# A transformer block on one core: the last MLP bias by an accumulating DMA, and one head moved from GpSimd to VectorE

## The reference

```python
x = x + attn_block(layernorm(x))
x = x + ffn(layernorm(x))

def attn_block(q_x):                      # q_x: normalized tokens
    xn = ln(q_x) * ln1_w + ln1_b
    q, k, v = xn @ wq + bq, xn @ wk + bk, xn @ wv + bv        # 16 heads of 16
    fq, fk = elu(q) + 1, elu(k) + 1
    # per token, over its heads h and the 16 x 16 features:
    kv    = einsum('bhnd,bhne->bnde', fk, v)
    attn  = einsum('bhnd,bnde->bhne', fq, kv) / (einsum('bhnd,bnd->bhn', fq, fk.sum(heads)) + 1e-6)
    x = q_x + attn @ wo + bo
    h = gelu((ln(x) * ln2_w + ln2_b) @ fc_w + fc_b)            # MLP 256 -> 1024
    return x + (h @ proj_w + proj_b)                           # MLP 1024 -> 256, the bias of this change

def ffn(x):                               # 8 experts, best two per token, and a shared MLP
    return silu(x @ sg_gate.T) * (x @ sg_up.T) @ sg_down.T + sum over two experts of weight * expert(x)
```

## Time and profile before

| what | value |
|---|---|
| median of three runs | 1758.97 us (1758.11 to 1759.81) |
| the profiled execution | 1756.6 us, of it 1754.7 us span |
| TensorE (PE) busy | 1682.2 us, 96% |
| VectorE (DVE) busy | 1176.5 us, 67% (nine tenths and more in the block loop) |
| GpSimd (POOL) busy | 1166.0 us, 66% |
| ScalarE (ACT) busy | 903.8 us, 52% |
| chain that ended last | PE 87%, ACT 5%, DVE 4%, issue 2% |
| DMA engines | mean 90 GB/s, one tenth busy in the block loop |

### The profile page before, as it was taken

The page is one execution under the profiler, slowest core; times in us unless marked ns, Lnnn a source line. Parts: engine busy times, 40 slices in busy tenths (PEclk is TensorE's granted clock), DMA queues, the critical chain, the costliest instruction groups (busy, mean ns, idle before and its releaser), DMA issues.

```text
span 1754.7 us, 25629 instructions
## 1 busy us (share of the span) xinstructions
PE 1682.2 (96%) x7243; PEld 1230.4 (70%) x7289; DVE 1176.5 (67%) x1967; ACT 903.8 (52%) x2240; POOL 1166.0 (66%) x624
## 2 busy tenths in 40 slices
PE   5888999999999999999999997989999999999997
PEld 3655665665665665665665664668888888888886
DVE  7999999999999999999999992222222222222221
ACT  4266667667667667667667636522232232232232
POOL 4779889889899899899889891314333333333333
PEclk9998999999999999999999998999999999999999
DMA  4211111111111111111111111166776766767774
GB/s 150 75 51 63 49 51 47 50 57 40 48 53 43 48 47 49 48 50 47 48 42 55 37 48 37 55 199 154 160 167 153 161 165 153 162 164 154 165 161 78
DMA packets 89455, 157.20 MB, mean 90 GB/s; under 512 B 8896, under 2 KB 72128, under 8 KB 89024
## 3 DMA queue, kind: packets, MB, share of 16 engines
q1 hardware_dynamic: 60512, 112.58, 20.6%
q0 software_dynamic: 28896, 44.06, 14.7%
HBM read 101.79 MB, written 48.56 MB: 86 GB/s over the span
## 4 chain that ended last, share of the span: by engine, by line
PE 87%; ACT 5%; DVE 4%; issue 2%; DMA 1%; SPq 1%; POOL 0%; POOLq 0%; ACTq 0%; DVEq 0%
PE p_b L1484 18%; PE p_b L1538 13%; PE p_b L1688 10%; PE p_b L1699 10%; PE p_b L1631 9%; PE p_q L1688 7%; PE p_q L1456 6%; PE p_v L1688 4%; PE p_v L1456 3%; PE p_b L1470 2%; PE p_xT L1675 2%; ACT rows L706 1%; ACT xmid L706 1%; PE p_xT L1616 1%; DVE prod L1014 1%
## 5 line engine op out<-in xcount | busy, mean ns | idle before, releaser
L654 POOL DMA_INDIRECT out_rows<-prod_pool,prod x142 | 221.2, 1558 | 385.8 <-ACT prod_pool L937 355.4
L523 POOL TENSOR_TENSOR prod_pool<-prod_pool 128x2048 f32<-128x2048 f32 (+1 forms) x180 | 347.6, 1931 | 15.1 <-DVE attn L1064 1.1
L1538 PE MATMUL p_b<-bT,fc_sb 128*128 128x512 f32 x512 | 231.1, 605 | 1.3 <-ACT bT L858 1.3
L1484 PE MATMUL p_b<-proj_sb,hid 128*128 128x256 f32 x1024 | 230.5, 379 | 0.0
L1484 PEld LDWEIGHTS p_b<-proj_sb,hid 128*128 128x128 f32 x1024 | 189.7, 190 | 29.4 <-issue 0.5
L1688 PE MATMUL p_b<-prod,exp_up 128*128 128x256 f32 x840 | 187.1, 379 | 0.0
L1014 DVE TENSOR_TENSOR prod<-p_q,eqk 128x4096 f32<-128x4096 f32 (+1 forms) x47 | 184.0, 3914 | 4.6
L1051 DVE TENSOR_REDUCE qkv<-prod 128x256 f32<-128x4096 f32 (+1 forms) x47 | 183.7, 3910 | 1.6
L1038 DVE TENSOR_TENSOR prod<-p_q,v_dve 128x2048 f32<-128x2048 f32 (+2 forms) x60 | 177.4, 2956 | 1.6
L1023 DVE TENSOR_REDUCE p_q<-prod 128x128 f32<-128x2048 f32 (+2 forms) x60 | 177.4, 2957 | 1.1
L574 POOL DMA_INDIRECT rows_sorted<-rows,slot x128 | 125.3, 979 | 79.0 <-issue 34.5
(11 more groups left out here) (207 smaller groups left out, 3005.3 us busy)
## 6 DMA issues: line engine op xcount, KB each, us to landing
exp_up<-in_experts SPq DMA_DIRECT2D x71, 768.0 KB, 4.6
prod<-rows_sorted SPq DMA_DIRECT2D x71, 260.0 KB, 2.8
xin<-in_x SPq DMA_DIRECT2D x16, 512.0 KB, 3.4
xres<-in_x SPq DMA_DIRECT2D x16, 512.0 KB, 3.8
xres<-xmid POOLq DMA_DIRECT2D x16, 512.0 KB, 4.6
out_rows<-x SPq DMA_DIRECT2D x16, 512.0 KB, 2.9
exp_dn<-in_experts SPq DMA_DIRECT2D x8, 384.0 KB, 5.5
out_rows<-prod_pool,prod POOLq DMA_INDIRECT x142, 3.8
```

The costliest lines, as they stand in the source:

```text
L523: done(g.tensor_tensor(prod_pool[:, at:at + n * w], prod_pool[:, at:at + n * w], prod_pool[:, at + n * w:at + 2 * n * w], ALU.add))
L654: pool.indirect_dma_start(out=out[:, :], out_offset=bass.IndirectOffsetOnAxis(ap=tok_i[j][:, a:a + 1], axis=0), in_=yg[j][:, a * D:(a + 1) ...
L1484: ins = t_.matmul(o, src[:, k, t * P:(t + 1) * P], w[:, k, :], start=k == 0, stop=bias_at is None and k == chunks - 1)
L1538: ins = t_.matmul(bnk[:], fc_sb[:, k, f * P:(f + 1) * P], bT[:, k, :], start=k == 0, stop=k == KC - 1)
```

## The change

The bias of the MLP's second layer (4*D) is no longer added by TensorE. Instead GpSimd adds it from DRAM to `xres` with one more accumulating DMA per block, once ScalarE has read `xres` (`a_ready`), and the DMA of `xmid` waits for that one to land (`xbias_added`) where it waited for the load of `xres`. The source is one row of 256 values, repeated over 128 partitions and four tiles. And `POOL_HEADS` goes from 6 to 5: VectorE takes eleven heads of the split tile in place of ten.

```diff
-POOL_HEADS = 6
+POOL_HEADS = 5
...
+        xbias_added = sem("xbias_added")
...
                 if core:
                     wait(pool, attn_ready, c)
                     done(halve(flat(s_pool[:, 0:HEADS, :])))
+                if stage_b:
+                    wait(pool, a_ready, TPB * c)
+                    stand_alone(pool)
+                    pool.dma_start(xres[:], b_tok[0:1, 4 * D:5 * D].unsqueeze(1).to_broadcast([P, TPB, D]),
+                                   accum_op=ALU.add).then_inc(xbias_added, 16)
                 if stage_d and stage_c:
                     gate_shared(c)
                 if stage_b:
 
-                    wait(pool, xres_loaded, 16 * c)
+                    wait(pool, xbias_added, 16 * c)
                     wait(pool, ln2_var, c)
                     stand_alone(pool)
                     pool.dma_start(xres[:].rearrange("p t d -> p (t d)"), xmid[:].rearrange("p t d -> p (t d)"),
...
-                    to_tokens(hid, FCH, proj_sb, (p_b0, p_b1), 4 * D, proj_psum,
+                    to_tokens(hid, FCH, proj_sb, (p_b0, p_b1), None, proj_psum,
                               at_last_chunk=lambda: wait(pe, gelu_ready, FCH * c),
                               between=next_x if more else None, per_bank=True)
```

## The result

The changed kernel takes 1823.09 us (1822.11 to 1823.65, four runs), the kernel before 1758.54 us on the same chip (1757.98 to 1759.81): 1.0365 times as long, 95% interval 1.0347 to 1.0383. The forecast was 1782 with a range up to 1806. The direction was right, the size was not: +64.5 us measured, +22.8 forecast. The profiled execution took 1822.1 us, its span 1820.1.

The account below looks back on a forecast made before the run. Two loops of waits (65.73 and 65.20 us) and TensorE's own 65.28 were taken as balanced; the loop through GpSimd would then set the block: 13 x 1.75 + 0.94 - 0.88 = +22.8 on 1758.97, so 1782 us, range 1768 to 1806.

Parts of the forecast that it names:

- First loop: VectorE to TensorE's next-tile projection and back through wo: 65.73 us a block, 66.80 after the change, 0.94 more than now.
- the head's 1.07: VectorE's four operations on the split tile with one more head: 4 x 0.267 = 1.07 us a block.
- the room of 0.13: Slack between the end of VectorE's last product (L1038) and TensorE's next projection (L1456): 0.13 us in the steady block.
- Removed matmuls: Four bias matmuls a block off TensorE, 0.44 us; pays only in first and last blocks, 0.88 us in all.
- Push of the gating product: New DMA ahead of L583 on GpSimd's queue delays it 0.58 + 1.56 = 2.14 us, and so TensorE's down-projection.
- 65.47: Loop VectorE, GpSimd gating product, TensorE, ScalarE, VectorE: 65.20 us plus 0.27 for the head, before the DMA's push.
- The second wait: GpSimd's wait for the bias to land before L621: landings up to some 8 us hidden, costed at nothing.
- The wait of TensorE: TensorE waits about 1.7 us before the down-projection in each of 13 blocks, released by GpSimd's gating product.

Follow-up runs that it names:

- the kernel that waits later: Changed kernel with the bias-landing wait and the second DMA moved behind the v products of tile 3, the bias DMA left in place: 1809.29 us.
- the larger pieces: Changed kernel with the bias standing four times in a row in DRAM, read as 128 pieces of 4 KB: 1795.0 us.
- with the clock's fall gone from eight of twelve blocks: Changed kernel, landing wait kept, with three extra products on TensorE ahead of its wait for the gating product: 1818.31 us.
- without both: Changed kernel with the landing wait moved later and three extra TensorE products ahead of its wait for the gating product: 1781.12 us.
- both moves and six heads: Changed kernel with bias DMA behind the gating product, landing wait and second DMA behind the v products, and six heads on GpSimd: 1781.86 us.

## Why the prediction was wrong

**First loop.** Right but for 0.11 us. +0.94 us a block was forecast; the head alone gave blocks of 66.91, which is 1.05 more, so nearly all of the head's 1.07 shows and the room of 0.13 that I had taken off was not there; +14.4 us in all against a forecast of 13. This loop did not set the block in the changed kernel.

**Removed matmuls.** Right as far as it can be told: 0.88 us was forecast for them, and leaving the bias out altogether changes nothing that can be measured.

**Push of the gating product.** Right. The DMA takes 1.42 us, where I took 1.56 between 0.97 and 3.88. From L534's end to the gating product's, the changed kernel takes 504.08 - 498.53 = 5.55 us, where before it was 0.17 + 3.44: a push of 1.94, with 2.14 forecast. The block that follows from it is there wherever nothing else is late: 65.47 + 1.94 = 67.41, and 67.45 was measured in the kernel that waits later; with the push of 1.49 of the larger pieces it is 66.96, and 66.98 was measured. The Trainium skill, "DMA: Bandwidth & Descriptors", section "Anatomy of one DMA — SWDGE (gpsimd) path", was weighed in the prediction with descriptor generation as small; the runs bear it out in part: 0.98 us for 128 pieces, 1.42 for 512, so four times as many cost 0.44 more.

**The second wait: this step failed.** I wrote: "A landing of up to some 8 us is hidden; I cost it at nothing." Beyond it "GpSimd would be the bound". The threshold was about right, although GpSimd comes to the wait 504.08 - 499.19 = 4.89 us after the issue and not 5.8: a landing of 6.2 us was hidden. The landing was not right: I had 4.6 us from L621 beside me and asked only how far it might grow, while for the DMA's own time I had taken care to bound what four times the pieces could do. The landing is 9.5 us, GpSimd stands 5.1 to 6.6 us a block, and its round becomes 70 to 71. A cost that was put at nothing with its cover named should have been carried into the range with the cover gone: my 1806 did not reach it.

**The wait of TensorE: the step that is missing.** I priced the 1.7 us that TensorE would wait at 1.7 us. Before the change TensorE was never idle that long in a steady block and the clock stood at 1.00 throughout, so the trace gave a wait no further price; it did hold TensorE's long waits of the first blocks, and the clock of those I did not read (0.92 and 0.89 over the two blocks before 197 us). With the wait the clock falls in every steady block of the changed kernel and in nine of twelve where only the landing wait is gone, and there a block that should take 67.45 takes about 70.7. The Trainium skill, "TensorE: Matmul & The Clock Gate", section "HAM oscillation — how this bites in real kernels", describes a loop in which each round waits, and each round starts slow again. The trace agrees in kind, with 0.95 to 0.98 granted over a steady block, but not in length: the waits here are 1.44 to 2.94 us (the blocks from 271 us on), and those of the section's kernel are 3 to 5 us. As a kind of loop it would have made a rival; from its lengths, a wait of 1.7 us would have been thought harmless.

The two do not add, since the longest loop sets the block: without the landing wait 1809.29, with the clock's fall gone from eight of twelve blocks 1818.31, without both 1781.12. Against the changed kernel that is 14, 5 and 42 us. The forecast of 1782 was the kernel without both.

## What to carry over

A DMA put on an engine's own queue costs in three places: what it pushes, what waits for its landing, and what is queued behind that wait; each needs its own price, and the landing of a new access pattern is not that of the nearest DMA in the trace. Where a fully busy TensorE is given even a short regular wait, ask what its clock does behind it: here a wait of 1.47 us cost another 3.3 where the clock fell. When two causes each suffice for a block, taking away either shows little, so take away both before you call one of them small.

## What the runs showed of the hardware

- An accumulating DMA of 512 KB in 1 KB pieces, all from one row of DRAM, landed in 9.5 us; from 512 rows in 6.2; in 4 KB pieces from one row in 5.2; the 4 KB one from SBUF in 4.6.
- Waits of TensorE of 1.45 to 2.2 us, once a block, behind 1.85 us of sixteen products of eight columns, came with a clock of 1.2 GHz in nine blocks of twelve and not in the other three, in one and the same kernel; no row shows what decides it. With both moves and six heads the clock fell even where the wait was 0.30 us. In the kernel before, with the same sixteen products and no wait, it fell in none of twelve.
- The gating product on GpSimd takes 4.02 us when it starts while the bias DMA is still being issued, 3.80 when that DMA has 128 pieces, and 3.42 when it does not.
